# Local attention with a window of 32: scores in blocks of 32 rows by 64 keys, two heads in a transpose

## The reference, cut to what matters

```python
def local_attention(q, k, v):              # window w = 32
    bq = q.reshape(b, h, nw, w, d)
    bk2, bv2 = look(bk), look(bv)          # the window before and its own: 64 keys
    mask = (it < jb) | (it > jb + w) | (jb == -1)
    sim = einsum('bhwie,bhwje->bhwij', bq, bk2) * QK_SCALE
    sim = where(mask, -finfo.max, sim)
    attn = softmax(sim, -1)
    out = einsum('bhwij,bhwje->bhwie', attn, bv2)
```

## Time and profile before

| | |
|---|---|
| median of 3 runs | 9056.33 us |
| the profiled execution | 9059.37 us, its span 9057.6 us |
| busy: PE, DVE, ACT, POOL | 78%, 66%, 60%, 46% |
| first and last mask of `L0f` | 702.6 and 5238.8 us |
| DMA over the whole span | 303.42 MB, mean 33 GB/s |

### The profile page before, as it was taken

The page is one execution under the profiler, slowest core; times in us unless marked ns, Lnnn a source line. Parts: engine busy times, 40 slices in busy tenths (PEclk is TensorE's granted clock), DMA queues, the critical chain, the costliest instruction groups (busy, mean ns, idle before and its releaser), DMA issues. The chain is left out here.

```text
span 9057.6 us, 216576 instructions
## 1 busy us (share of the span) xinstructions
PE 7063.8 (78%) x72628; PEld 4785.1 (53%) x72628; DVE 5994.4 (66%) x12697; ACT 5416.0 (60%) x13778; POOL 4204.8 (46%) x3731
## 2 busy tenths in 40 slices
PE   5768888888888888888888849997888847743357
PEld 2325665665655566566566638886555523322245
DVE  6886776777767767677676736666666758854432
ACT  4446877777777777787777834443676744512112
POOL 4555555555555555555555524445444435532000
PEclk8889999999999999999999969999999978866578
DMA  3220000000000000000000020000000032232001
GB/s 127 117 89 14 11 10 22 11 9 21 13 10 18 14 10 11 21 11 10 20 14 9 11 74 5 5 5 12 18 18 17 14 110 117 116 106 73 20 0 28
DMA packets 154026, 303.42 MB, mean 33 GB/s; under 512 B 23512, under 2 KB 106800, under 8 KB 134256
## 3 DMA queue, kind: packets, MB, share of 16 engines
q1 hardware_dynamic: 145472, 270.86, 9.3%
q10 hardware_dynamic: 1584, 15.21, 0.4%
q0 software_dynamic: 6144, 5.25, 0.4%
HBM read 208.74 MB, written 32.18 MB: 27 GB/s over the span
## 5 line engine op out<-in xcount | busy, mean ns | idle before, releaser
L822 ACT ACTIVATE L0f_scores<-L0f_scores,L0f_nmx,L0f_rn 128x128 f32<-128x128 f32 x3072 | 1338.0, 441 | 60.4 <-DVE L0f_nmx L926 59.8
L1008 PE MATMUL L0f_ring<-L0f_wqkv,L0f_hT 128*128 128x512 f32 x2324 | 1210.3, 627 | 110.2 <-DMA L0f_scales<-L_ffn_scales_dram 60.3
L752 POOL TENSOR_TENSOR L0f_qr<-L0f_qs,L0f_table 128x512 f32<-128x512 f32 x776 | 990.8, 1277 | 498.7 <-ACT L0f_qs L793 420.4
L759 POOL TENSOR_TENSOR L0f_qr<-L0f_qr,L0f_m 128x512 f32<-128x512 f32 x776 | 987.3, 1272 | 280.0 <-issue 137.8
L766 POOL TENSOR_TENSOR L0f_qr<-L0f_qr,L0f_rn 128x512 f32<-128x512 f32 x388 | 396.7, 1044 | 762.2 <-DVE L0f_rn L918 625.8
L924 DVE TENSOR_REDUCE L0f_mx<-L0f_scores 128x8 f32<-128x1024 f32 x384 | 469.5, 1223 | 363.2 <-PE L0f_scores L1036 175.5
L895 DVE TENSOR_TENSOR L0f_m<-L0f_ring,L0f_table 128x512 f32<-128x512 f32 x776 | 521.9, 688 | 271.4 <-ACT L0f_qs L793 250.6
L822 ACT ACTIVATION_READ_ACCUMULATOR L0f_scores<-L0f_scores,L0f_nmx,L0f_rn 128x1 f32 x3072 | 662.0, 215 | 0.0
L837 ACT ACTIVATE L0f_oT<-L0f_o 128x512 f32<-128x512 f32 x385 | 235.0, 610 | 632.4 <-PE L0f_o L1074 591.1
L1008 PEld LDWEIGHTS L0f_ring<-L0f_wqkv,L0f_hT 128*128 128x128 f32 x2324 | 391.4, 195 | 393.1 <-issue 287.8
L936 DVE TENSOR_TENSOR L0f_prob<-L0f_scores,L0f_sums 128x512 f32<-128x512 f32 x768 | 531.5, 692 | 61.7 <-issue 5.4
(11 more groups left out here) (540 smaller groups left out, 19262.0 us busy)
## 6 DMA issues: line engine op xcount, KB each, us to landing
L0a_bc_all<-L0a_bc_rows SPq DMA_DIRECT2D x32, 2048.0 KB, 11.3
L2a_bc_all<-L2a_bc_rows SPq DMA_DIRECT2D x32, 2048.0 KB, 11.4
L0f_vmix<-L0f_vb SPq DMA_DIRECT2D x288, 128.0 KB, 2.3
L1f_vmix<-L1f_vb SPq DMA_DIRECT2D x96, 128.0 KB, 2.3
L0f_wqkv<-L_ffn_wqkv_dram SPq DMA_DIRECT2D x7, 1536.0 KB, 6.0
L2f_parts<-L2f_zero ACTq DMA_DIRECT2D x8, 1088.0 KB, 11.4
n_s<-mixer_out SPq DMA_DIRECT2D x32, 256.0 KB, 4.9
L2f_back<-L2f_parts SPq DMA_DIRECT2D x32, 256.0 KB, 3.5
```

Source lines behind the costliest of these rows:

```text
L752: e.tensor_tensor(rotated, qs[:, q % QN], spread(cos, 1, 8), ALU.mult).then_inc(cosed.sem, 1)
L759: e.tensor_tensor(rotated, rotated, m2[:, q % SN], ALU.add).then_inc(added.sem, 1)
L822: a = e.activation(s_ps[:, h, j], s_ps[:, h, j], ACT.Exp, bias=nmx[:, s, col:col + 1], scale=rn[:, tt, 2 * u, col:col + 1], accum_out=sums ...
L1008: e.matmul(bank[:], hT[:, tt * P:tt * P + P], wqkv[:, col:col + 512], start=True, stop=True).then_inc(full, 1)
```

## The change

`L0f` gets a function of its own, `narrow_attention_net`; `L1f` keeps the old one. The new function is the old one with the window fixed at 32 and these parts replaced (lines with - are those of `local_attention_net`, lines with + those of the new function):

```diff
-        kT = r.sb("kT", [P, TT, pairs, P])
-        vb = r.sb("vb", [P, 2, heads, DH])
-        vmix = r.sb("vmix", [P, 2, heads, DH])
-        prob = r.sb("prob", [P, 2, 2, GP, P])
-        pT = r.sb("pT", [P, 2, 2, GP, P])
+        kT = r.sb("kT", [P, pairs, W + SEQ])
+        vb = r.sb("vb", [P, 2, 2, pairs, DH])
+        vmix = r.sb("vmix", [P, 2, NB - 1, pairs, DH])
+        prob = r.sb("prob", [P, 2, GP, 2 * KEYS])
+        pT = r.sb("pT", [P, 2, GP, P])
...
-        s_ps = r.ps("scores", [P, 2, GP, P])
-        pt_ps = r.ps("pt", [P, 2, GP, P])
+        both_ps = r.ps("scores", [P, 2, 2, 512])
+        s_ps = both_ps[:, :, :, 0:GP * KEYS].rearrange("p s h (j k) -> p s h j k", j=GP)
+        pt_ps = both_ps[:, :, :, 512 - 2 * P:512].rearrange("p s b (j q) -> p s b j q", j=2)
...
-                    e.dma_start(vmix[0:window, own], vb[0:window, own]).then_inc(mixed, 16)
-                    e.dma_start(vmix[P - window:P, own], vb[P - window:P, before]).then_inc(mixed, 16)
+                    for h in range(2):
+                        at = h * DH
+                        if tt:
+                            e.dma_start(vmix[at:at + W, own, 0], vb[P - W:P, before, h]).then_inc(mixed[tt], 16)
+                        e.dma_start(vmix[at + W:at + KEYS, own, 0], vb[0:W, own, h]).then_inc(mixed[tt], 16)
+                        e.dma_start(vmix[at:at + KEYS, own, 1], vb[W:W + KEYS, own, h]).then_inc(mixed[tt], 16)
+                        e.dma_start(vmix[at:at + KEYS, own, 2], vb[DH - at:DH - at + KEYS, own, h]).then_inc(mixed[tt], 16)
 
                 def mix_all(it):
-                    for tt in range(1, TT):
+                    for tt in range(TT):
                         mix(it, tt)
...
-                            e.activation(pT[:, parity(key), 0], pt_ps[:, 0], ACT.Copy).then_inc(unflipped[0].sem, 1)
+                            e.activation(pT[:, parity(key)].rearrange("p (b j) q -> p b j q", b=2), pt_ps[:, parity(key)],
+                                         ACT.Copy).then_inc(unflipped.sem, 1)
...
-                            e.wait_ge(*flipped(it, key + (i,), 4))
-                            e.wait_ge(*exped(it, key + (i,)))
+                            e.wait_ge(*flipped(it, key, 2))
+                            e.wait_ge(*exped(it, key))
+                            e.reciprocal(sums[:, s], sums[:, s])
+                            e.drain()
+                            e.tensor_tensor(prob[:, s].rearrange("p j (h k) -> p h j k", h=2), s_ps[:, s], spread(sums[:, s], 3, KEYS),
+                                            ALU.mult).then_inc(scaled.sem, 1)
...
-                            e.wait_ge(*scaled(it, key + (1,), 2))
+                            e.wait_ge(*unflipped(it, key, 2))
...
                             for j in range(GP):
+                                for i in range(NB):
+                                    rows, cols = slice(i * W, i * W + W), slice(tt * P + i * W, tt * P + i * W + KEYS)
+                                    for h in range(2):
+                                        half = slice(h * DH, h * DH + DH)
+                                        a = e.matmul(s_ps[rows, s, h, j], qT[half, tt % 2, GP * u + j, rows],
+                                                     kT[half, GP * u + j, cols], start=False, stop=j == GP - 1)
...
-                                e.wait_ge(*unflipped[i](it, key, 1))
-                                for j in range(GP):
-                                    a = e.transpose(pt_ps[:, i, j], prob[:, s, i, j], g.ident[:])
+                            for j in range(GP):
+                                a = e.transpose(pt_ps[:, s, j // 2, j % 2], prob[:, s, j], g.ident[:])
...
                             for j in range(GP):
+                                for i in range(NB):
+                                    cols = slice(i * W, i * W + W)
                                     for h in range(2):
+                                        half = slice(h * DH, h * DH + DH)
+                                        if i == 2 * h + 1:
+                                            values = vb[half, par, h, GP * u + j]
+                                        else:
+                                            values = vmix[half, par, (0, 2, 1, 2)[i], GP * u + j]
+                                        a = e.matmul(o_ps[half, j, cols], values, pT[half, s, j, cols], start=True, stop=True)
```

More of the change, by code:

```diff
@@ L221, in window_mask, with narrow_window_mask @@
     return np.where(both, 0.0, MASKED).astype(mybir.dt.np(BF16))
+def narrow_window_mask():
+    window = 32
+    row = (np.arange(P) % window)[:, None]
+    key = np.arange(2 * window)[None, :]
+    own = (key >= row) & (key <= row + window)
+    first = own & ((np.arange(P) >= window)[:, None] | (key >= window))
+    both = np.stack([np.concatenate([first] * 4, 1), np.concatenate([own] * 4, 1)], 1)
+    return np.where(both, 0.0, MASKED).astype(mybir.dt.np(BF16))
 def by_partition(a, p=P):
@@ L3178, in build @@
         mamba_net(nc, g, "L0a", nets["L0_attn"], center=False, residual=False)
-        local_attention_net(nc, g, "L0f", 16, 32, 6, nets["L0_ffn"])
+        narrow_attention_net(nc, g, "L0f", 16, 6, nets["L0_ffn"])
         combine(nc, g, "n1", x, x_dram, True, True)
@@ L3215 @@
         laid_out[net]["rope"] = rotary_constants(window)
-        laid_out[net]["mask"] = window_mask(window)
+        laid_out[net]["mask"] = narrow_window_mask() if window == 32 else window_mask(window)
     nets = {net: {k: dram(f"{net}_{k}_dram", a) for k, a in ws.items()} for net, ws in laid_out.items()}
```

644 lines of the change are left out of this document (added).

## The result

| | before | with the change |
|---|---|---|
| median | 9055.60 us (4 runs, 9054.25 to 9063.38) | 8982.21 us (4 runs, 8973.39 to 8985.67) |
| ratio | | 0.9916, interval 0.9899 to 0.9933 |
| the profiled execution | | 8985.67 us, span 8983.9 |
| first and last mask of `L0f` | | 703.4 and 5164.2 us |

The change is faster by 73 us, or 0.8%; 94 us were forecast. The stage of `L0f` (first to last mask) shrinks by 75.4 us, so the whole gain lies in it: 92.9 us a sequence in place of 94.5. Lines of the changed kernel have other numbers: masks L1034, score L1040, flip L1048, value L1071, projection L1014, norm L946, ScalarE's copy of transposed weights L841.

A forecast was written before the change was run, and what follows sets the result against it. TensorE's own work sets the pace, with each group waiting some tenths on VectorE. 46 + 31 + 16 - 167 - 20 = -94 us takes 9059 to 8965 us; range 8740 to 9130, the forecast's own 8900 to 9030.

The forecast's parts named there:

- Passes: TensorE's masks, score, flip and value in `L0f`: score and value passes at about 22.4 ns, together +46 us.
- The rule weighed against it: Skill's 60 cycles a matmul: a 32-column product costs 25 ns, making the TensorE sum some 130 us higher.
- Rival 1: Score and value passes are cheaper, 17.3 ns: 251 us more goes, 8714 or 8740 us; chance 0.17.
- 2 (dearer): Score and value passes cost 2.9 ns more each, and the kernel is slower: 9119 us; chance 0.16.
- Slow clock: First tile's score and a value after each loop return run at clock 0.50, so their extra costs again: +31 us.
- Rival 4: The slow clock lasts longer after a return: 5 us at half speed loses 105 us, 9070 us; chance 0.07.
- The mixes: Eight transfers replace two; six more issues delay the next layer's weights by 3.3 us at five layer changes: +16 us.
- Waits on norm and copy: TensorE's waits for VectorE at masks, transposes and value, 167 us in the stage, all go: -167 us.
- Rival 3: The waits move: TensorE waits for a projection's bank behind the norm instead; 9152, or 9059 with half; chance 0.12.
- a pass beyond 24 ns: Profile sign that the forecast is wrong; at 24.1 ns a pass the -94 us is used up.
- The shift's wait: The feed-forward shift's wait for the residual add, 38.7 us, a round trip of which half goes: -20 us.
- Late next: What would be late once these waits are gone: the return's own stall and ScalarE, at 78%.

The follow-up runs named there:

- run 1: The changed kernel with score loops reordered so eight passes in a row use the same 64 x 32 part of the array: 9431.62 us.
- run 7: The changed kernel with value products ordered heads outermost, 32 passes in a row on one 64 x 64 part of the array: 9913.96 us.
- run 5: The changed kernel without value products for the last two 32-row query blocks, the others cut in two of 32 output rows: 8696.7 us.
- run 4: The changed kernel with every value product cut in two of 32 output rows, 128 passes a group instead of 64: 9170.91 us.
- run 9: The changed kernel with the next layer's query, key and value weights issued ahead of the last mix: 8950.04 us.
- run 3: The changed kernel with the masks again waiting for VectorE's norm of the group before: 8991.71 us.
- run 11: The changed kernel with two sequences written out per turn of the loop, 2 jumps back a layer instead of 6: 8788.56 us.
- run 8: The changed kernel with value products on four 64 x 64 parts of the array in turn instead of two, same number of instructions: 8775.64 us.
- run 6: The changed kernel with value products of two of four pairs of heads cut in two, 96 passes a group: 9041.55 us.
- run 12: The changed kernel with value on four array parts, weights issued ahead of the last mix, and two sequences a turn: 8569.64 us.

## Why the prediction was right, and where it wasn't

The sign, the range and the size held (−73 for −94), but the inside of the sum did not: large errors of opposite sign cancelled, and that the size came out is luck. TensorE's time over the whole stage (first to last mask, counted like the table above, with waits of over 0.15 us as idle time, all rounded) says which:

| us in the stage | forecast | measured |
|---|---|---|
| masks, score | −81, +163 | −96, −91 |
| flip, value | −169, +132 | −203, +328 |
| slow clock, in blocks not rewritten | +31 (for the rewritten ones) | +64 (projections +18, output products +46) |
| wait for the next layer's weights | +16 | +22 |
| waits for norm and copy | −167 | −80 |
| the shift's wait | −20 | −2 |
| other waits, other work | 0 | +1, −19 |
| sum | −94 | −75 |

- **Passes (+46 us): the step that failed.** One price, 22.4 ns, was taken for score and value alike, since two unlike rows showed it. A pass has no such price. On one part of the array it takes 37 ns (64 x 32, run 1) or 58 ns (64 x 64, run 7); work on n parts in turn divides that, down to 10 to 12 ns. Score goes over eight parts: 12.3 ns. Value goes over two: 31. The old 32-column passes at 22.5 ns used 128 rows of the array, another case. In a later tile score gave 0.28 us where +0.36 was forecast, and value cost 0.87 where +0.32 was. In the whole stage the four blocks together give 61 us, and that with their own share of the slow clock, where +46 and +31 were forecast.
- **The rule weighed against it.** The Trainium skill ("TensorEngine Tiling (Array Packing)", "Instruction Overhead") has about 60 cycles for each matmul, an estimate of 25 ns at 2.4 GHz. No row bears this out as a floor: 12.3, 16.7 and 10.6 ns a pass were measured, and even the two passes of a product together take only 21.2 ns in run 5. Its warning against small pieces holds in another way: run 4 was slower for its number of instructions.
- **Rival 1 (cheaper) and 2 (dearer)** both came true, one for score, one for value. The first named the cause in passing (eight places rather than four) and gave value the same gain without counting value's places.
- **Slow clock (+31).** The two stretches of 12 us behind a return's masks (columns as above) read so in the change, where the masks start at 1073.84:

```profile
1072.00:1084.00 12.00, 8.14 (x136) 6.23 (x137) 4.02 (x14) 1.84 (x5) 3.57 (x4) 0.55 0.02 4
1084.00:1096.00 12.00, 10.99 (x110) 7.68 (x109) 6.04 (x18) 8.00 (x26) 3.75 (x6) 0.88 0.16 44
```

  and so before, where they start at 1079.91:

```profile
1078.00:1090.00 12.00, 8.68 (x83) 6.25 (x84) 3.26 (x12) 2.62 (x9) 2.04 (x2) 0.57 0.01 3
1090.00:1102.00 12.00, 9.66 (x84) 6.37 (x84) 8.31 (x21) 9.79 (x31) 5.92 (x8) 1.00 0.11 23
```

  Over the 41 returns of the stage the clock is back 12.4 us behind the masks' start in place of 7.0 (medians), and time at half clock, from the mean clocks 0.952 and 0.930, goes from 434 to 626 us, 4.7 us more a return. 507 of 3072 passes of the output products now fall into it instead of 56 and take 217 ns each instead of 116; with the projections that is the +64 us. The term was too small: it counted the added passes, not that the work behind them is pushed into the slow stretch. Rival 4, with 5 us at half clock, was close in size, and its loss was hidden by the errors on the other side; the warning that the clock would be at 0.50 past the first projections came true.
- **The mixes (+16)** measured 3.65 us at each change of layer, 22 us in six; run 9 got 32 us back by issuing the load earlier. The term had five such places, and there are six, since the last layer loads weights too.
- **Waits on norm and copy (−167): half of it failed.** Of 154.6 us 81.4 stay (46.5 + 34.9), 73 are gone. Most of the masks' part was given back a step later in the chain (run 3). What stays is mostly one wait each in a sequence, 20 to 30 us behind its start. It does not hang on the return's stall: in run 11 value's wait stands as often and as long in sequences that start without a stall (23 times, 23.6 us) as in those with one (21 times, 21.5 us). What it hangs on was not tested. Rival 3 named the right effect, waits that move, at the wrong place: TensorE's waits on `L0f_m` fell from 19.3 to 6.6 us. The recorded sign that TensorE would wait more on ScalarE's copies came true (46.5 us at value, where it waited for none before), as did the one of a pass beyond 24 ns.
- **The shift's wait (−20)** did not move: 38.7 and 37.5 us. Less other work on VectorE doesn't shorten this round trip. "Late next" was right in naming the return's stall, 4.2 us a sequence before: taking out 24 jumps gave 194 us (run 11). It missed the other large gain, value's two parts (207 us, run 8).
- **VectorE's load** fell from 70 to 57% of the stage, where 53% was forecast, and was worth nothing by itself, as forecast (columns as above, before and change):

```profile
702.60:5238.80 4536.20, 3954.65 (x43160) 2722.50 (x43160) 3167.14 (x7208) 3505.72 (x10100) 2443.93 (x2151) 0.95 0.06 14
703.40:5164.20 4460.80, 3939.79 (x63087) 2860.76 (x63088) 2562.84 (x6060) 3319.31 (x10099) 2438.75 (x2151) 0.93 0.14 39
```

## What to carry to other kernels

Price a small matmul by the part of the array that it uses and count how many different parts come in turn; with 58 ns on a 64 x 64 part, two parts give 31 ns and four 16.7, for the order of the loops, the place of the output and, here, weights loaded with halves swapped and a second copy. Dense small passes also empty the supply of instructions, once there are many in a row (96 and 128 here), so gain parts by placing pieces, not by cutting them smaller. Don't count a wait as saved before asking whether the next step in the same chain meets it, and look first at the stall that the change leaves alone: 24 jumps back fewer gave 194 us here, the whole change 73.

## What was not expected of the hardware

- A pass takes 12.3 ns over eight parts, 10.6 over four of 64 x 32, 16.7 over four of 64 x 64, 31 over two, 58 over one. With 64 columns on one 64 x 32 part (changed every eight passes) it is 36.6 ns, with 32 columns on one 64 x 64 part 58: the width of the weights weighs more than the columns of the data. Why was not tested.
- The granted clock fell from 1.00 to 0.53 in the middle of a block in which TensorE was busy without a gap, all of it on one quarter of the array (run 7); in the other traces every fall had a wait of TensorE shortly ahead of it. Why was not tested.
- TensorE stands 1.0 to 2.4 us inside dense passes in 32 of 385 blocks of 96 of them (run 6) and in 186 of 385 blocks of 128 (run 4); with 64 in a block this was seen three times, in run 12. Every such stop of runs 4 and 6 ends 1.2 to 1.7 us after a block of instructions has landed.
- A jump back costs TensorE 3.7 and 2.0 us of standing still and, in the change, a stretch of 12 us at half clock (9 us in the kernel before); writing out two sequences a turn gave 194 us for 24 jumps fewer, 8 us a jump.
